# One shared batch ahead of the routed chunks in an attention and mixture-of-experts kernel

## The reference

```python
xn = _layernorm(x, axis=-1)
# attention: 16 heads of 16, causal, Q/K/V = relu(xn @ W + b), then
out = softmax(scores) @ V + xn; attn = gamma * layernorm(out) + beta
# experts, on the 8192 rows of xn
shared_out = (silu(xf @ sw1) * (xf @ sw3)) @ sw2
logits = xf @ router_w.T + experts_bias
rw, sel = jax.lax.top_k(logits, 2); rw = softmax(rw)
moe_out = sum over the two chosen experts e of rw_e * (silu(xf @ w1[e]) * (xf @ w3[e])) @ w2[e]
result = x + attn + moe_out + shared_out
```

## Time and profile before

| | |
|---|---|
| profiled execution | 1862.29 us |
| its span, first to last instruction | 1860.5 us |
| TensorE busy | 1713.3 us, 92% |
| VectorE, ScalarE, GpSimd busy | 68%, 59%, 63% |
| mean granted TensorE clock | 0.975 of full speed |
| attention | to about 908 us |
| experts' stage | from 913.16 us |
| its loop, per step | 17.78 us |
| half steps, most of them | about 9.7 us |

### The profile page before, as it was taken

The page is one execution under the profiler, slowest core; times in us unless marked ns, Lnnn a source line. Parts: engine busy times, 40 slices in busy tenths (PEclk is TensorE's granted clock), DMA queues, the critical chain, the costliest instruction groups (busy, mean ns, idle before and its releaser), DMA issues.

```text
span 1860.5 us, 35897 instructions
## 1 busy us (share of the span) xinstructions
PE 1713.3 (92%) x12070; PEld 1288.1 (69%) x12070; DVE 1271.4 (68%) x3089; ACT 1088.8 (59%) x2066; POOL 1169.2 (63%) x1435
## 2 busy tenths in 40 slices
PE   3489999998999899999799999999999999999998
PEld 2245555555555555555478888888888898888887
DVE  6788888888889888877375445445544544566666
ACT  5247567666677666666556666666666675333332
POOL 4466557776777677745466767777777685543443
PEclk9689999999999999999799999999999999999999
DMA  1434445544544445453755666657567673544543
GB/s 54 152 122 122 132 127 172 159 154 152 157 150 155 147 155 168 143 189 132 267 184 166 215 198 218 209 185 234 191 195 230 188 241 132 175 147 147 157 147 99
DMA packets 244225, 310.30 MB, mean 167 GB/s; under 512 B 31467, under 2 KB 209269, under 8 KB 237941
## 3 DMA queue, kind: packets, MB, share of 16 engines
q1 hardware_dynamic: 231796, 274.98, 46.2%
q0 software_dynamic: 12288, 33.57, 5.6%
HBM read 209.60 MB, written 98.34 MB: 166 GB/s over the span
## 4 chain that ended last, share of the span: by engine, by line
PE 18%; POOL 16%; issue 11%; DVE 2%; ACT 2%; POOLq 1%; DMA 0%; SPq 0%; DVEq 0%
PE gu L1959 11%; PE yp L1973 6%; POOL early_low L1626 3%; POOL w_up_l L1626 2%; POOL rows L1653 2%; POOL rows L1658 2%; POOL rows L1687 2%; POOL early_down L1626 1%; POOL w_dn_l L1626 1%; PE xt L1948 1%; POOL sm L1669 1%; DVE hf L1819 1%; ACT hid_h L1726 1%; DVE passed L1863 1%; ACT sil L1724 0%
## 5 line engine op out<-in xcount | busy, mean ns | idle before, releaser
L655 ACT ACTIVATE pT<-st_ps 128x512 f32<-128x512 f32 x682 | 368.5, 562 | 263.4 <-PE st_ps L1265 256.3
L925 DVE CUSTOM_DVE_ANT_0 s_ps<-s_ps,masks 128x384 f32<-128x384 f32 (+1 forms) x512 | 314.4, 632 | 37.4 <-PE s_ps L1244 32.0
L1959 PE MATMUL gu<-xc,w_up_h 128*128 128x512 f32 (+1 forms) x1120 | 336.0, 383 | 1.5 <-POOL w_up_l L1626 1.0
L1819 DVE TENSOR_TENSOR hf<-sil,gu 128x512 f32<-128x512 f32 (+1 forms) x220 | 143.5, 652 | 269.5 <-ACT sil L1724 269.2
L1244 PE MATMUL s_ps<-k_aug,q_aug 97*128 97x512 bf16 (+3 forms) x1024 | 261.8, 308 | 37.7 <-DVE mx L925 23.7
L1263 PE MATMUL st_ps<-q_aug,k_aug 99*128 99x512 bf16 (+1 forms) x992 | 269.3, 304 | 11.5 <-ACT pT L655 6.4
L1822 DVE TENSOR_TENSOR hid_l<-hf,hid_h 128x512 fp32r<-128x512 f32 (+1 forms) x220 | 170.6, 776 | 147.6 <-ACT hid_h L1726 147.6
L1726 ACT ACTIVATE hid_h<-hf 128x512 fp32r<-128x512 f32 (+1 forms) x220 | 133.0, 605 | 180.5 <-DVE hf L1819 180.5
L1959 PEld LDWEIGHTS gu<-xc,w_up_h 128*128 128x128 f32 x1120 | 203.8, 189 | 45.6 <-issue 6.1
L1724 ACT ACTIVATE sil<-gu 128x512 f32<-128x512 f32 (+1 forms) x220 | 123.8, 563 | 188.8 <-PE gu L1959 188.7
L1634 POOL DMA_INDIRECT got<-expert_results,place x128 | 122.1, 954 | 159.4 <-DVE hf L1819 137.6
(11 more groups left out here) (259 smaller groups left out, 4026.8 us busy)
## 6 DMA issues: line engine op xcount, KB each, us to landing
early_raw<-in_L_ffn_w_dram SPq DMA_DIRECT2D x60, 512.0 KB, 6.4
w_raw<-in_L_ffn_w_dram SPq DMA_DIRECT2D x57, 512.0 KB, 5.6
part_scr<-parts SPq DMA_DIRECT2D x64, 384.0 KB, 3.9
q_aug<-part_scr SPq DMA_DIRECT2D x192, 128.0 KB
k_aug<-part_scr SPq DMA_DIRECT2D x192, 128.0 KB
early_raw<-expert_rows SPq DMA_DIRECT2D x34, 512.0 KB, 3.9
expert_results<-yo SPq DMA_DIRECT2D x32, 512.0 KB, 3.3
x_sb<-in_L_attn_x_dram SPq DMA_DIRECT2D x16, 512.0 KB, 4.5
```

What stands on the lines that cost most here:

```text
L655: fn(pT[j][:, h:h + heads], unit_view(column_bank(b, u), heads, w), ACT.Exp).then_inc(exp_done, 1)
L925: vec.tensor_tensor_reduce(bank[:, 0:keys], bank[:, 0:keys], masks[:, 2 * C + P - keys:2 * C + P], 1.0, LOWEST, ALU.add, ALU.max, mx[:, h ...
L1819: vec.tensor_tensor(hf[:, m % 2, 0:w], sil[:, m % 2, 0:w], gu[m % 2][:, 1, 0:w], ALU.mult).then_inc(h_done, 1)
L1959: last = mm(gu[m % 2][:, a, 0:width(n)], w_up[wpar][x][:, a, c, P * m:P * (m + 1)], xc[par][:, y, c, 0:width(n)], start=k == 0, stop=k == ...
```

## The change

The experts' stage begins with one batch of the shared expert. Step 0 takes batch 0 of xn and the weights sw1, sw3 and sw2, which don't depend on the routing; steps 1 to 39 are the 39 routed chunks, and steps 40 to 54 the shared batches 1 to 15. The weights and rows of step 0 are loaded and cut in iteration B-2 of attention instead of B-1. VectorE adds the result of step 0 to x of batch 0 and it is stored as `first_sum`; the final layernorm of batch 0 takes it in place of x. In step 0 ScalarE cuts the weights of step 1 behind tiles 1, 2 and 3. The places are worked out behind the tiles of the seven half steps. The gates are worked out in the last iteration of attention.

```diff
@@ attention, SyncE
-                await_(sp, table_ready, 1)
-                sp.reg_load(first_reg, plan["expert"][0:1, 0:1])
-                for a, (n, rows_) in enumerate((("w1", C), ("w3", C), ("w2", 2 * C))):
+                for a, (n, rows_) in enumerate((("sw1", C), ("sw3", C), ("sw2", 2 * C))):
...
-                if i == B - 1:
+                if i == B - 2:
                     load_early()
+                    load_early_rows()
@@ attention, GpSimd and ScalarE
-                if i == B - 1:
+                if i == B - 2:
                     for q in range(PIECES):
                         early_low(q)
...
+                    if i == B - 1 and s == AT_GATE_EXP:
+                        await_(act, gate_differs, 1)
+                        fn(plan["gate"][:, 1], plan["gate"][:, 0], ACT.Exp).then_inc(gate_grown, 1)
-                    if i == B - 1 and s in AT_HIGH:
+                    if i == B - 2 and s in AT_HIGH:
                         early_high(AT_HIGH.index(s))
@@ experts, SyncE
+                first = known(pair) and pair == 1
+                if first:
+                    sp.wait_ge(y_stored, 16)
+                sp.dma_start(out_res, (first_sum if first else t["x"][pair - 1]).rearrange("(t p) c -> p t c", p=P)
...
+            sp.dma_start(acc[:, 0], t["x"][0].rearrange("(t p) c -> p t c", p=P)).then_inc(first_in, 16)
...
+            load_x(2, chunk_rows(2))
+            load_routed(2, 0)
@@ experts, ScalarE
+            def first_step():
+
+                tile(0, 0, 0)
+                x_high(1, 1)
+                for m in range(1, NH):
+                    tile(0, 0, m)
+                    cut_high(1, 1, (2 * m - 2, 2 * m - 1))
@@ experts, VectorE
+            PLACES = (((1, 2), ()), ((3, 4), ()), ((5, 6), ()), ((7,), (0,)), ((), (1, 2)), ((), (3, 4, 5)), ((), (6, 7)))
+            def add_first():
+
+                dve.wait_ge(first_in, 16)
+                dve.wait_ge(y_ready, 1)
+                vec.tensor_tensor(yo[:], yp[:], acc[:, 0], ALU.add).then_inc(y_out, 1)
...
-                if known(r) and r in (0, 1, 2, 3):
-                    rest_places([0, 1, 2, 7][r:r + 1])
+                if width(n) < S:
+                    regions, rests = PLACES[n - 1 - WHOLE]
+                    region_places(regions)
+                    rest_places(rests)
...
-            region_places()
+            first_step()
             routed(dve, routed_step)
@@ experts, GpSimd
+            cut_low(1, 1)
             pool.wait_ge(params_in, 32)
             routed(pool, step)
```

More of the change, by code:

```diff
@@ L312, in _ @@
         def _(sp):
-            end_reg, first_reg = (ctx.enter_context(sp.register(n)) for n in ("end", "first"))
+            end_reg = ctx.enter_context(sp.register("end"))
             wst = qf[:].rearrange("p a (c n) -> p a c n", c=NC)
@@ L1472, in routed @@
         def routed(engine, step):
[L1479 to L1480 removed]
+            for n in range(1, 5):
+                step(n, n % 2, (n + 1) // 2, 1 if n >= 3 else None)
             with engine.Fori(2, B) as pair:
[L1482 to L1485 removed]
+                for odd in range(2):
+                    step(pair * 2 + odd + 1, 1 - odd, pair + 1, pair)
+            for n in range(WHOLE + 1, CHUNKS + 1):
+                step(n, n % 2, None, B if n < WHOLE + 3 else None)
         def shared(step):
[L1490 removed]
+            for c in range(1, B):
                 step(CHUNKS + c, (CHUNKS + c) % 2, c)
@@ L1687, in norm_end, with step @@
                 gp.tensor_tensor(out_whole, out_y, out_res, ALU.add).then_inc(norm_read, 1)
-            def step(r, par, begins, ends):
-                if par == 1 and begins is not None:
+            def step(n, par, begins, ends):
+                if par == 0 and begins is not None:
                     norm_sum(begins)
-                cut_low(r + 1, 1 - par, (0, 1))
-                if par == 0 and ends is not None:
+                cut_low(n + 1, 1 - par, (0, 1))
+                if par == 1 and ends is not None:
                     norm_end(ends)
-                if par == 1 and begins is not None:
+                if par == 0 and begins is not None:
                     norm_root(begins)
-                cut_low(r + 1, 1 - par, range(2, PIECES))
-                if par == 1 and begins is not None:
+                cut_low(n + 1, 1 - par, range(2, PIECES))
+                if par == 0 and begins is not None:
                     norm_beta(begins)
+            cut_low(1, 1)
             pool.wait_ge(params_in, 32)
@@ new lines, in routed_step @@
+            def routed_step(n, par, begins, ends):
+                if width(n) < S:
+                    cut_high(n + 1, 1 - par, (0, 1))
+                    tile(n, par, 0)
+                    x_high(n + 1, 1 - par)
+                    cut_high(n + 1, 1 - par, (2, 3))
+                    if par == 1 and ends is not None:
+                        norm_scale(ends)
+                    act.wait_ge(y_ready, n)
+                    cut_high(n + 1, 1 - par, (4, 5))
+                    tile(n, par, 1)
+                    copy_result(n - 1)
+                    tile(n, par, 2)
+                    tile(n, par, 3)
@@ L1749, in routed_step @@
                     return
-                tile(r, par, 0)
-                x_high(r + 1, 1 - par)
-                cut_high(r + 1, 1 - par, (0, 1))
-                if par == 0 and ends is not None:
+                tile(n, par, 0)
+                x_high(n + 1, 1 - par)
+                cut_high(n + 1, 1 - par, (0, 1))
+                if par == 1 and ends is not None:
                     norm_scale(ends)
-                if par == 1 and begins is not None:
+                if par == 0 and begins is not None:
```

227 lines of the change are left out of this document (108 added, 119 removed).

## The result

The changed kernel took 1865.60 us (median of 14 runs, 1862.92 to 1869.00) against 1863.01 us of the kernel before on the same chips (14 runs, 1860.31 to 1865.64): a ratio of 1.0016, 95% interval 1.0008 to 1.0023, so 1.5 to 4.3 us slower. That is just inside the 0.2% called "same": slower, as forecast, but by less. The forecast was 1868.5, the range 1858 to 1876; the likeliest outcome in it, a slowdown beyond 0.2% (0.60), did not come.

A forecast was written before the change was run, and what follows sets the result against it. TensorE was taken to bound the experts' loop, so only its waits could move. Terms -4.9 + 4.0 - 7.9 + 10.5 + 3.9 = +5.6 us on 1862.29 gave 1867.9, or 1868.5 against the median; range 1858 to 1876.

The forecast's parts named there:

- Term 1: End of attention: the wait for the routed weights goes, score blocks are no longer late; -4.9 us, ends 1.0 and 5.4 saved.
- Rival D: End of attention: the fills hold the store of y, so 1.0 us is saved instead of 4.9; 1872.4 us, chance 0.08.
- Term 2: Step 0: weights cut one tile later, so TensorE waits for the low parts and loses clock; +4.0 us, ends 2.0 and 5.0.
- Term 3: Four written-out routed steps: place operations between their tiles go, and with them most of the excess; -7.9 us, ends -5 and -8.9.
- Term 4: Half steps: added place operations wait for GpSimd's subtractions, 2.1 us reaches TensorE in five of seven steps; +10.5 us.
- Term 5: First completion of batch 0, a step earlier with gathers unmoved: TensorE waits for hf and loses clock; +3.9 us, ends 0 and 5.
- Rival A: Half steps: place operations fit into the room there, costing 1.8 us instead of 10.5; 1859.8 us, chance 0.18.
- Rival B: First completion: the first gathers are ready, by sooner issue or landing, so its +3.9 us goes; 1864.6 us, chance 0.14.
- Rival C: Half steps: TensorE's 2 us waits bring the clock down, 6.5 us more; 1875.0 us, chance 0.12.

The follow-up runs named there:

- late_load: Changed kernel with step 0's weights and rows loaded and cut in attention's last iteration again, without the wait for the table: 1865.57 us, ratio 1.0012 to the kernel before.
- table_wait: late_load with the old wait for the table before the weights' load added back: 1868.03 us, ratio 1.0022 to the kernel before.
- table_wait_rows: table_wait with step 0's rows also loaded as before, behind the eight fills and ahead of y's store: 1869.09 us, ratio 1.0034 to the kernel before.
- cut_order: Changed kernel with step 0's cuts of the next weights put ahead of tiles 1, 2 and 3 instead of behind: 1860.77 us, ratio 0.9990 to the kernel before.
- places_back: Changed kernel with place operations where they were: seven pairs ahead of the first tile, the others in the first four steps: 1864.52 us, ratio 1.0004 to the kernel before.
- places_hidden: Changed kernel with place operations moved out of the half steps, ahead of step 0's first tile and behind the sixth half step: 1855.86 us, ratio 0.9957 to the kernel before.
- hold_cut: Changed kernel with GpSimd's first pair of subtractions in half steps made to wait for the step's first hf: 1856.73 us, ratio 0.9963 to the kernel before.
- gather_early: Changed kernel with batch 0's gathers no longer waiting for products of the first full shared step: 1862.57 us, ratio 1.0001 to the kernel before.
- shared_early: places_hidden, cut_order and gather_early together, plus the later batches' shared weights loaded at the sixth half step's start: 1850.44 us, ratio 0.9934 to the kernel before.
- shared_early_places: shared_early with four last place pairs behind the last half step, four behind the first shared step's rows: 1843.68 us, ratio 0.9891 to the kernel before.

## Why the prediction was right, and where its sizes were off

The sign and place of all five terms were right. The mechanism was right for terms 2 and 4, half right for 1, and for 3 and 5 right except for a part of each. The time, 1865.6 against 1868.5, was 2.9 us too high, for these reasons.

- **Term 1** was mis-sized: 4.9 foretold, 5.8 by the marks from a common block, above my upper end of 5.4. The step between the PV blocks and the block of 3.21 us gave back the 3.9 and 1.5 us; the cuts in the earlier iteration cost 0.8 where I charged 0.5; the quicker end behind y, 1.2 us, I had put at nothing. The reasoning was half right: I took the move to the earlier iteration for a part of the cause. late_load shows that the move is worth 0.7 us by the marks and nothing by the times, table_wait that the wait for the table is worth 2 to 4, and table_wait_rows that with the rows it is worth about 4. Rival D, the fills that hold the store of y, was real but small in the changed kernel (y ready at 904.19, stored at 904.84).
- **Term 2**: 2.5 us more waiting (2.75 for 0.24) and 1.7 us of clock, as worked out (2.5 and 1.5). cut_order shows the cause.
- **Term 3** was mis-sized: I left 1.0 us of the excess in place, and none stayed. The four intervals are 17.68, 17.69, 17.68 and 17.85, under the loop's 17.78 on the mean. Its cause was right in part: the two operations of the earlier trace rows waited for subtractions, but the four slowest of the kernel before (2.30 to 2.42 us) each stood behind one operation of the layernorm on GpSimd, and 3.7 us of the 8.9 came with a hid_l that did so (see places_back).
- **Term 4** was 2.1 us for five steps and measured 2.23: hf came 2.22 us late, not 2.4, but all of it reached TensorE. The sequence (first operation free, two that wait, the last free) came out as written in four of the five, and in the first the first two waited. places_hidden and hold_cut show that next to nothing else is in it. The Trainium skill ("SBUF — State Buffer", section "Who interferes with whom") has VectorE and GpSimd lock a shared pair of ports, the one that issues first for its whole instruction; and it has a VectorE instruction with two inputs in SBUF contend with a GpSimd instruction that reads SBUF, one with at most one such input not, unless it runs in a mode that uses both ports. The runs agree with the second: hid_l of a half step stretches from 0.42 to as much as 1.47 us and the place operation with two such inputs from 0.29 to about 1.3, while hf, whose one operand is in PSUM, stays at 0.41 or 0.42 beside the same subtractions. The other place operation, with one tensor input, stretches too; whether it ran in such a mode no run shows. Of the first they show who goes next: each of the 85 place operations in the 14 profiles that took over 0.5 us ended 0.08 to 0.15 us after exactly one GpSimd instruction did.
- **Term 5** was mis-sized: +3.9 foretold, about 2.57 in eight of the nine profiles that keep the gathers. The wait of VectorE is there (5.1 us), and of the 2.8 us by which I had hf late TensorE saw 2.2 to 2.3: the last gather of the batch landed 2.7 us after its issue instead of 3.0, and the operations behind it took 5.1 instead of 5.3. The 1.1 us for the clock were paid in one profile alone, the first (4.15); in the others the clock stayed at 1.00 after the same wait. I had taken the fall of the clock for certain.
- **Rival A** (places fit) was wrong in each of the seven profiles that have them there with the subtractions beside them (intervals 11.9 to 12.2). **Rival B** did not happen by itself but is what gather_early makes. **Rival C** fell: the granted clock in the first five half steps is 1.00.

Terms 1, 3 and 5 are 0.9, 1.25 and 1.3 us off in the same direction, and term 4 takes 0.7 of that back. The sixth half-step interval, which I had at nothing, moved by +1.23 in one profile and by -0.83 in the next, with the clock. The measured "same" (within 0.2%) had a chance of 0.26 in the forecast, since the whole of the sum lay within 2 us of that bound.

## What to carry to other kernels

A short operation is not priced by its length but by what the other engine on its port does in that moment: here four operations of 0.29 us cost 2.2 us a step beside two subtractions, nothing that the intervals show where GpSimd stood idle, and 0.2 to 0.5 us where it was made to wait for the next hf. Before work is moved into "free" time, look at which wait makes that time free, since the next edit may remove it (shared_early). When a dependence is removed together with a move, try the two apart: here the move was worth 0.7 us by the marks and nothing by the times. And a stall of 2 us has no fixed price: with the same wait the clock fell in one execution and not in the next.

## What the runs showed that was not expected

- The same attention code ended at very different times: the first transposes of the experts' stage came at 905.15 us in cut_order and at 911.08 in shared_early_places, whose programs up to there are the same. A single profile can't tell a change of 3 us; marks from a common block can. The spread of the times goes with the clock: of the changed kernel's 14 runs, the seven up to 1864.94 us have a mean granted clock of 0.978 to 0.980 and those from 1866.25 us on 0.974 to 0.978.
- Three place operations in places_back, and four in the kernel before, took 2.3 to 2.4 us, twice the length of a subtraction. Each stood behind one GpSimd operation of the layernorm, on 128x1024 values, not behind two subtractions (VectorE, then GpSimd):

```profile
974.83 2.41 DVE L1890 TENSOR_SCALAR passed<-slot_f,turns 128x128 f32<-128x128 f32 x1
...
974.31 2.84 POOL L1680 TENSOR_TENSOR rows<-rows,beta_b 128x1024 f32<-128x1024 f32 x1
```
